# Attention with a post-norm and a quantised FFN: probabilities divided in three PSUM row buffers, rotary products taken from PSUM, no swap DMAs

## The chip, the cores and the metric

One NeuronCore of a Trainium2 chip runs the whole program in one launch. The metric is the device time of one execution in microseconds. The kernel before takes 2369.5 us (median of 3 executions, 2362.24 to 2372.11).

## The reference

```python
def layer(x, Wq, bq, Wk, bk, Wv, bv, Wo, bo, gate/up/down int8 weights and scales):   # x: (4, 1024, 256) f32
    q, k, v = heads(x @ Wq + bq) * 128 ** -0.5, heads(x @ Wk + bk), heads(x @ Wv + bv)  # 16 heads of 128
    q = q * cos + rotate_half(q) * sin          # rotate_half: (-second half, first half) of the 128 dims
    k = k * cos + rotate_half(k) * sin
    attn = softmax(causal(q @ k.T))             # 1024 x 1024 per head
    x = layernorm(x + (attn @ v) @ Wo + bo)
    return layernorm(x + ((silu(x @ Wg * sg) * (x @ Wu * su)) @ Wd) * sd)
```

There are 4 x 16 = 64 heads. The time is in them: the last 220 us are the FFN.

## The kernel before

**Precision by halves.** Matrix products are made in a fast rounded format. So each operand is kept as a rounded high part and the low rest, and each product is three matmuls (high x high, high x low, low x high). The high part is made by ScalarE (a copy that rounds), the low part by VectorE or GpSimd (the value less the high part). Probabilities and V use float16 parts, scaled by powers and bounds; the rest uses rounded float32.

**The loop.** `sequence_timelines` calls `run(n, ...)` once per head n = -1 ... 64 on every engine; each engine has its own copy of the loop body, written out by hand in 8 slots s = 0 ... 7. Every engine does its instructions in order; semaphores join them. During head n, slot s works on the 128-query row block s of head n (s+1 blocks of 128 keys, causal), and beside it lie the projections of head n+1 (s < 4), the product with V of head n-1 (`ATTEND`), and, once per pair of heads, the V projection and the output projection.

**A row block.** TensorE makes the scores in a PSUM buffer S[s % 2] of two banks (L1139). VectorE adds the mask and takes the negated maximum, and writes the row to SBUF, `p_row` (L878). ScalarE takes Exp in place with its row sum (L686), then writes the high part of the undivided probabilities, times 2^15, to `planes` (L694). VectorE writes the low part from `p_row` and `planes` (L888). A DMA on SyncE's queue transposes `planes` into `PT` (L393, `turn`), of which there are three planes in turn. The S buffer is free as soon as L878 has read it.

**The product with V.** `attend` (L1103) gathers in PSUM O[g], g = 0, 1 for the two halves of 512 queries. The division by the row sums comes here: `reciprocal` (L936, L939) makes four columns at a time, SyncE sends them to DRAM (L401) and spreads them back over all partitions as `recip_b` (L406), and `normalise_output` (L906) multiplies O[g] by it into `norm_o`. ScalarE rounds that (L528, `output_high`) and GpSimd makes the rest (L482).

**The projections and the rotary part.** `chunk` (L1156) makes a 128 x 512 piece of q or k of the next head in the upper bank of S[c % 2]. ScalarE adds the bias and takes it to SBUF, `rot` (`chunk_out`, L702). SyncE copies the two halves of 64 partitions crosswise into `swap` by two DMAs (L384, `swap_halves`). GpSimd multiplies `swap` by the sine (L452), VectorE `rot` by the cosine (L929), GpSimd adds them (L444), ScalarE rounds the sum into QK (L528) and GpSimd makes the rest (L468).

**The other PSUM users.** V pieces go through bank PJ (L1173; read by ScalarE L614 and VectorE L897), the output projection through WP (L1121; added to `resid` by VectorE L922). The bound for V's scale and the fold of bv into bo are small matmuls in WP.

## Time and profile before

| | |
|---|---|
| median of 3 executions | 2369.5 us |
| the profiled execution, and its span | 2372.22 us, 2370.4 us |
| busy TensorE, VectorE, ScalarE, GpSimd | 1929.0, 1984.0, 1375.0, 1619.6 us |
| mean granted TensorE clock | 0.908 of 2.4 GHz |
| mean busy share of the 16 DMA engines over the heads | 0.69 |

How to read it: "busy" is the union of an engine's instructions; instructions issued back to back overlap by about 0.1 us in the records, so sums of durations come out a little higher than the busy time. "Idle before" is the time in which an engine had nothing to do just ahead of an instruction, and the arrow names what ended it. The scores of head 0 start at 31.0 us, those of head 63 end soon after 2150 us.

### The profile page before, as it was taken

The page shows a single profiled execution, that of the slowest core. Times are in us where ns is not written, and L with a number is a line of the kernel's source. Part 1 is how long each engine was busy: PE and PEld are TensorE (multiplying, and loading weights), DVE is VectorE, ACT ScalarE, POOL GpSimd, SP SyncE. Part 2 cuts the span into 40 slices and gives each one's busy share as a digit, 9 for nine tenths or more (in the row PEclk, how much of TensorE's full clock was granted, in tenths as well). Part 3 has the DMA queues.
Part 4 walks back from the last instruction along what each step waited for, and adds up shares of the span by engine and source line. Part 5 has one row for each costly group of instructions (what it writes and reads, how often), then busy time and mean ns, then how long its engine had stood idle before and what let it go on. Part 6 is the DMA issues. An engine that isn't in the chain of part 4 may idle for free. (4 is left out here: it accounts for less than half of the span.)

```text
span 2370.4 us, 35295 instructions
## 1 busy us (share of the span) xinstructions
PE 1929.0 (81%) x10464; PEld 1515.4 (64%) x10464; DVE 1984.0 (84%) x2981; ACT 1375.0 (58%) x2718; POOL 1619.6 (68%) x1169
## 2 busy tenths in 40 slices
PE   5787887877888888878888878778888878878998
PEld 4566666656666666656666666656666656656887
DVE  6788888888888888888888888888888888985786
ACT  3655565655665665655666656565666656664443
POOL 4567766766677767777777777676667766773554
PEclk9899898899988998889888899889988998999999
DMA  4766777667767776767666677667766787664001
GB/s 113 175 131 125 144 156 128 128 146 152 135 134 144 139 160 133 140 139 156 142 137 135 137 157 145 127 139 151 139 132 132 144 174 150 134 125 98 19 19 36
DMA packets 716092, 311.09 MB, mean 131 GB/s; under 512 B 638080, under 2 KB 650880, under 8 KB 714496
## 3 DMA queue, kind: packets, MB, share of 16 engines
q1 hardware_dynamic: 692224, 266.88, 56.8%
q10 hardware_dynamic: 23680, 41.95, 6.4%
q8 instruction: 87, 1.43, 0.3%
q14 instruction: 101, 0.83, 0.1%
HBM read 81.95 MB, written 8.65 MB: 38 GB/s over the span
## 5 line engine op out<-in xcount | busy, mean ns | idle before, releaser
L686 ACT ACTIVATE p_row<-p_row,neg_max 128x128 f32<-128x128 f32 (+7 forms) x512 | 396.1, 774 | 598.5 <-DVE neg_max L878 589.6
L888 DVE SCALAR_TENSOR_TENSOR planes<-p_row,planes 128x128 f16<-128x128 f32 (+7 forms) x512 | 644.2, 1258 | 42.9 <-ACT planes L694 42.8
L452 POOL TENSOR_TENSOR swap<-swap,sin_t 128x512 f32<-128x512 f32 x256 | 383.5, 1499 | 217.3 <-DMA swap<-rot 217.2
L878 DVE CUSTOM_DVE_ANT_0 p_row<-S,mask_row 128x128 f32<-128x128 f32 (+7 forms) x512 | 385.0, 752 | 132.8 <-PE S L1139 116.1
L929 DVE TENSOR_TENSOR rot<-rot,cos_t 128x512 f32<-128x512 f32 x256 | 353.0, 1379 | 105.8 <-DMA swap<-rot 100.1
L444 POOL TENSOR_TENSOR rot<-rot,swap 128x512 f32<-128x512 f32 x252 | 351.4, 1394 | 71.5 <-DVE rot L929 71.4
L694 ACT ACTIVATE planes<-p_row 128x128 f16<-128x128 f32 (+7 forms) x512 | 347.3, 678 | 25.6 <-DMA PT<-planes 17.5
L1139 PE MATMUL S<-QKA 128*128 128x512 f32 (+4 forms) x1152 | 287.6, 378 | 75.8 <-issue 43.8
L1173 PE MATMUL PJ<-WV,xT 128*128 128x256 f32 x1500 | 234.1, 313 | 109.5 <-DVE VB L897 53.5
L1139 PE MATMUL S<-QKB 128*128 128x512 f32 (+4 forms) x1152 | 303.5, 394 | 16.0 <-ACT rot L702 9.2
L1173 PEld LDWEIGHTS PJ<-WV,xT 128*128 128x128 f32 x1500 | 221.7, 218 | 134.6 <-DVE VB L897 62.6
L1139 PEld LDWEIGHTS S<-QKA 128*128 128x128 f32 x1152 | 196.4, 197 | 119.9 <-issue 93.7
L1121 PE MATMUL WP<-WO,OTA 128*128 128x256 f32 x768 | 152.9, 313 | 145.9 <-DVE resid L922 134.7
L1103 PE MATMUL O<-PT,VB 128*128 128x512 f16 (+3 forms) x1152 | 242.0, 345 | 6.0 <-DMA PT<-planes 6.0
L1139 PEld LDWEIGHTS S<-QKB 128*128 128x128 f32 x1152 | 213.6, 212 | 51.9 <-issue 21.2
L1103 PE MATMUL O<-PT,VA 128*128 128x512 f16 (+3 forms) x1152 | 240.2, 343 | 4.8 <-DMA PT<-planes 4.8
L1121 PEld LDWEIGHTS WP<-WO,OTA 128*128 128x128 f32 x768 | 127.1, 214 | 165.2 <-issue 158.8
L1156 PE MATMUL S<-xT,WA 128*128 128x512 f32 x768 | 211.9, 414 | 10.5 <-DVE xT L738 8.8
L468 POOL TENSOR_TENSOR QKB<-rot,QKB 128x512 fp32r<-128x512 f32 x128 | 206.9, 1623 | 18.8 <-ACT QKB L528 18.8
L468 POOL TENSOR_TENSOR QKA<-rot,QKA 128x512 fp32r<-128x512 f32 x124 | 207.5, 1674 | 13.1 <-ACT QKA L528 12.6
L1156 PE MATMUL S<-xT,WB 128*128 128x512 f32 x768 | 202.4, 399 | 9.7 <-ACT rot L702 9.7
L702 ACT ACTIVATE rot<-S,bias_m 128x512 f32<-128x512 f32 x256 | 172.4, 674 | 25.5 <-PE S L1156 19.3
(142 smaller groups left out, 3156.7 us busy)
## 6 DMA issues: line engine op xcount, KB each, us to landing
swap<-rot SPq DMA_DIRECT2D x512, 128.0 KB, 2.6
recip_b<-recip_d SPq DMA_DIRECT2D x128, 256.0 KB, 4.1
w_raw<-in_w_heads ACTq DMA_DIRECT2D x64, 256.0 KB, 3.0
wv_raw<-in_w_heads ACTq DMA_DIRECT2D x32, 256.0 KB, 2.7
PT<-planes SPq DMA_TRANSPOSE x512, 3.7
wo_raw<-in_wo_heads ACTq DMA_DIRECT2D x32, 256.0 KB, 3.0
attn_d<-resid ACTq DMA_DIRECT2D x4, 1024.0 KB, 5.5
x_raw<-in_x_cols SPq DMA_DIRECT2D x3, 1024.0 KB, 6.0
```

What stands on the lines that cost most here:

```text
L444: nc.gpsimd.tensor_tensor(rot[:, c, :], rot[:, c, :], swap[:, c, :], ALU.add).then_inc(rot_done, 1)
L452: nc.gpsimd.tensor_tensor(swap[:, c, :], swap[:, c, :], sin_t[:, half], ALU.mult).then_inc(sin_done, 1)
L468: nc.gpsimd.tensor_tensor(q[:, c % 2, 1, half], rot[:, c, :], q[:, c % 2, 0, half].bitcast(F32), ALU.subtract).then_inc(rot_lo, 1)
L686: nc.scalar.activation(row, row, ACT.Exp, bias=neg_max[:, s:s + 1], scale=-1.0, accum_out=row_sum[:, s:s + 1]).then_inc(exped, 1)
L694: nc.scalar.activation(row_halves(n, s)[:, 0], p_row[:, k % 2, 0:cols].rearrange("p (j q) -> p j q", q=P), ACT.Copy, scale=UP).then_inc(hi ...
L878: nc.vector.tensor_tensor_reduce(row_view(p_row[:, k % 2, 0:cols], s), score_view(S[s % 2], s), row_view(mask_row[:, N - cols:], s), -1.0, ...
L888: nc.vector.scalar_tensor_tensor(halves_of[:, 1], p_row[:, k % 2, 0:cols].rearrange("p (j q) -> p j q", q=P), UP, halves_of[:, 0], ALU.mul ...
L929: nc.vector.tensor_tensor(rot[:, c, :], rot[:, c, :], cos_t[:, half], ALU.mult).then_inc(cos_done, 1)
L1103: last = mm(O[g][:, first * P:], V[buf][:, pv, j, who], PT[g][:, j, pp, first:, :].rearrange("p i q -> p (i q)"), start=j == 0 and z == 0, ...
L1139: last = mm(S[s % 2][:, z * GQ:z * GQ + b - a], QK[par][:, 0, part_q, s * P:(s + 1) * P], QK[par][:, 1, part_k, a:b], start=(part_q, part_ ...
L1156: last = mm(S[c % 2][:, GQ:], W[nxt][:, c % 2, pw, t, :], xT[:, px, t, half], start=i == 0 and t == 0, stop=i == 2 and t == KT - 1)
L1173: last = mm(v_psum(n, i)[:, t2, :], xT[:, px, t, tok], WV[:, pw, t, :, :].rearrange("p h c -> p (h c)"), start=z == 0 and t == 0, stop=z = ...
```

## The change

What it does: (1) there are three S buffers of two banks, used in turn by row number (`row_psum`), and one bank O and one bank X in place of O0, O1, WP and PJ. (2) Exp writes into the row's S buffer, no longer in place in SBUF; the reciprocal is taken per row block, 128 x 1, right after Exp, and the division is in the scale of the high part and of the low part, both read from PSUM. So S is held from the scores until the low part is made. (3) `normalise_output`, the DRAM round trip and GpSimd's `output_low` go; ScalarE and VectorE take the two parts straight from O. (4) The two DMAs per chunk go; ScalarE's copy of a chunk becomes two copies of 64 partitions that swap the halves, and VectorE's cosine product reads the chunk in PSUM and adds the bias. (5) The score scale moves to L878, and the bias copy goes. (6) Output projection, V pieces, fold and bound get other slots, all through X, and `ATTEND` is redistributed.

```diff
-    S = [pb("S0", N), pb("S1", N)]
-    O = [pb("O0", GQ), pb("O1", GQ)]
-    WP = pb("WP", GQ)
-    PJ = pb("PJ", GQ)
+    S = [pb(f"S{i}", N) for i in range(3)]
+    O = pb("O", GQ)
+    X = pb("X", GQ)
+    def row_psum(n, s):
+        return S[(8 * n + s) % 3]
...
-        return ({2: 2, 7: 3} if par else {5: 0, 7: 1}).get(s) if makes_v(n) else None
+        return ({1: 0, 7: 1} if par else {1: 2, 3: 3}).get(s)
...
-        slots = {1: 1, 5: 2, 6: 3} if par else {6: 0}
+        slots = {3: 2, 5: 3} if par else {5: 0, 7: 1}
...
-    ATTEND = {0: [(0, 0), (0, 1)], 1: [(0, 2), (0, 3)], 3: [(1, 0), (1, 1)], 4: [(1, 2), (1, 3), (1, 4)],
-              5: [(1, 5)], 6: [(1, 6)], 7: [(1, 7)]}
+    ATTEND = {0: [(0, 0), (0, 1), (0, 2), (0, 3)], 3: [(1, 0)], 4: [(1, 1), (1, 2), (1, 3)], 5: [(1, 4)],
+              6: [(1, 5), (1, 6), (1, 7)]}
...  SyncE: swap_halves and reciprocals are gone, turn stays
...  GpSimd: output_low is gone; WO's rest moves from slot 0 to 2, WV's from 2 to 5
-                        pool.wait_ge(swapped[c], 32 * (m + 1))
+                        pool.wait_ge(chunk_sb, 2 * n_four(m, c))
...  ScalarE, at the head of slot s: output_high in slots 1 and 7, value_high of slot s-1's piece; then
-                nc.scalar.activation(row, row, ACT.Exp, bias=neg_max[:, s:s + 1], scale=-1.0,
+                nc.scalar.activation(row_psum(n, s)[:, 0:cols], p_row[:, k % 2, 0:cols], ACT.Exp,
+                                     bias=neg_max[:, s:s + 1], scale=-1.0,
                                      accum_out=row_sum[:, s:s + 1]).then_inc(exped, 1)
...
-                act.wait_ge(exped, k + 1)
+                act.wait_ge(recip_ok, k + 1)
                 wait(act, turned_in[k % 3], 16 * (k // 3))
-                nc.scalar.activation(row_halves(n, s)[:, 0], p_row[:, k % 2, 0:cols].rearrange(
-                    "p (j q) -> p j q", q=P), ACT.Copy, scale=UP).then_inc(high, 1)
+                nc.scalar.activation(row_halves(n, s)[:, 0], row_psum(n, s)[:, 0:cols].rearrange(
+                    "p (j q) -> p j q", q=P), ACT.Copy, scale=recip[:, s:s + 1]).then_inc(high, 1)
...
-                nc.scalar.activation(rot[:, c, :], S[c % 2][:, GQ:], ACT.Identity,
-                                     bias=bias_m[:, m_par, c % 2:c % 2 + 1],
-                                     scale=SCALE if c % 2 == 0 else 1.0).then_inc(chunk_sb, 1)
+                for lo, hi in ((0, D // 2), (D // 2, 0)):
+                    nc.scalar.activation(swap[lo:lo + D // 2, c, :], row_psum(n, c)[hi:hi + D // 2, GQ:], ACT.Identity,
+                                         bias=bqk[hi:hi + D // 2, c % 2, m % H:m % H + 1]).then_inc(chunk_sb, 1)
...  VectorE, order within slot s: add_output of slot s-1's piece, masked_scores(s), probs_low(s-1),
...  output_low (s = 1, 7), value_low, reciprocal(s), scale_up, rotate_cos(s-1)
-                wait(dve, low, k - 1)
-                wait(dve, exped, n_scored(n - 1, s))
+                wait(dve, exped, k - 1)
...
-                nc.vector.scalar_tensor_tensor(halves_of[:, 1], p_row[:, k % 2, 0:cols].rearrange(
-                    "p (j q) -> p j q", q=P), UP, halves_of[:, 0], ALU.mult, ALU.subtract).then_inc(low, 1)
+                nc.vector.scalar_tensor_tensor(halves_of[:, 1], row_psum(n, s)[:, 0:cols].rearrange(
+                    "p (j q) -> p j q", q=P), recip[:, s:s + 1], halves_of[:, 0], ALU.mult, ALU.subtract
+                    ).then_inc(low, 1)
...
+            def output_low(h, g):
...
+                nc.vector.scalar_tensor_tensor(OT[q][:, 1, o], O[:, :], pv_down[:, slot:slot + 1],
+                                               OT[q][:, 0, o].bitcast(F32), ALU.mult, ALU.subtract
+                                               ).then_inc(o_lo, 1)
...
-                nc.vector.tensor_tensor(rot[:, c, :], rot[:, c, :], cos_t[:, half], ALU.mult).then_inc(cos_done, 1)
+                dve.wait_ge(chunk_sb, 2 * n_four(m, c))
+                wait(dve, rot_lo, n_four(m - 1, c))
+                nc.vector.scalar_tensor_tensor(rot[:, c, :], row_psum(n, c)[:, GQ:], bqk[:, c % 2, m % H:m % H + 1],
+                                               cos_t[:, half], ALU.add, ALU.mult).then_inc(cos_done, 1)
...
+            def reciprocal(n, s):
+                dve.wait_ge(exped, n_scored(n, s))
+                nc.vector.tensor_scalar(sum_down[:, s:s + 1], row_sum[:, s:s + 1], 1.0 / UP, None, ALU.mult
+                                        ).then_inc(summed_down, 1)
+                dve.wait_ge(summed_down, n_scored(n, s))
+                nc.vector.reciprocal(recip[:, s:s + 1], sum_down[:, s:s + 1]).then_inc(recip_ok, 1)
...  TensorE, scores(s)
-                    wait(pe, maxed, n_scored(n, s) - 2)
-                    if s >= 4:
-                        wait(pe, chunk_sb, n_four(m, s % 2 + 2) if project else 0)
+                    k = n_row(n, s)
+                    wait(pe, low, k - 2)
+                    if project and 4 <= s < 7:
+                        pe.wait_ge(cos_done, n_four(m, s - 3))
```

## Rows read from the trace of the kernel before

**Rows 1.** From the page: span, busy time, granted clock and DMA, packets.

```profile
span 2370.4 us, 35295 instructions
PE 1929.0 (81%) x10464; PEld 1515.4 (64%) x10464; DVE 1984.0 (84%) x2981; ACT 1375.0 (58%) x2718; POOL 1619.6 (68%) x1169
...
DMA packets 716092, 311.09 MB, mean 131 GB/s; under 512 B 638080, under 2 KB 650880, under 8 KB 714496
```

**Rows 2.** Busy time by stretch, ahead of, over and behind the heads.

```profile
core 0: us, PE busy (x) PEld busy (x) DVE busy (x) ACT busy (x) POOL busy (x), PEclk, DMA share, GB/s
0.00:31.00 31.00, 15.76 (x76) 13.41 (x77) 17.20 (x26) 10.31 (x18) 8.38 (x11) 0.96 0.47 143
31.00:2150.00 2119.00, 1711.40 (x9222) 1328.58 (x9222) 1805.59 (x2622) 1268.76 (x2551) 1501.26 (x1075) 0.90 0.69 141
2150.00:2370.00 220.00, 201.82 (x1169) 173.40 (x1168) 161.20 (x335) 95.97 (x151) 110.01 (x84) 0.98 0.14 38
```

**Rows 3.** Costliest groups of the page: row work and rotary work, all shapes together.

```profile
L686 ACT ACTIVATE p_row<-p_row,neg_max 128x128 f32<-128x128 f32 (+7 forms) x512 | 396.1, 774 | 598.5 <-DVE neg_max L878 589.6
L888 DVE SCALAR_TENSOR_TENSOR planes<-p_row,planes 128x128 f16<-128x128 f32 (+7 forms) x512 | 644.2, 1258 | 42.9 <-ACT planes L694 42.8
L452 POOL TENSOR_TENSOR swap<-swap,sin_t 128x512 f32<-128x512 f32 x256 | 383.5, 1499 | 217.3 <-DMA swap<-rot 217.2
L878 DVE CUSTOM_DVE_ANT_0 p_row<-S,mask_row 128x128 f32<-128x128 f32 (+7 forms) x512 | 385.0, 752 | 132.8 <-PE S L1139 116.1
L929 DVE TENSOR_TENSOR rot<-rot,cos_t 128x512 f32<-128x512 f32 x256 | 353.0, 1379 | 105.8 <-DMA swap<-rot 100.1
L444 POOL TENSOR_TENSOR rot<-rot,swap 128x512 f32<-128x512 f32 x252 | 351.4, 1394 | 71.5 <-DVE rot L929 71.4
L694 ACT ACTIVATE planes<-p_row 128x128 f16<-128x128 f32 (+7 forms) x512 | 347.3, 678 | 25.6 <-DMA PT<-planes 17.5
L1139 PE MATMUL S<-QKA 128*128 128x512 f32 (+4 forms) x1152 | 287.6, 378 | 75.8 <-issue 43.8
...
L1139 PE MATMUL S<-QKB 128*128 128x512 f32 (+4 forms) x1152 | 303.5, 394 | 16.0 <-ACT rot L702 9.2
...
L702 ACT ACTIVATE rot<-S,bias_m 128x512 f32<-128x512 f32 x256 | 172.4, 674 | 25.5 <-PE S L1156 19.3
```

**Rows 4.** Groups of VectorE, shapes apart.

```profile
L906 DVE TENSOR_TENSOR norm_o<-O,recip_b 128x512 f32<-128x512 f32 x128 | 137.7, 1076 | 0.0
L936 DVE TENSOR_SCALAR sum_up<-row_sum,pv_up 128x4 f32<-128x4 f32 x128 | 131.9, 1031 | 0.0
L878 DVE CUSTOM_DVE_ANT_0 p_row<-S,mask_row 128x512 f32<-128x512 f32 x64 | 43.6, 681 | 0.9 <-PE S L1139 0.8
L939 DVE RECIPROCAL recip<-sum_up 128x4 f32<-128x4 f32 x128 | 22.8, 178 | 4.4
```

**Rows 5.** Single lines of VectorE and GpSimd: durations in ns, least/median/most.

```profile
L897 DVE SCALAR_TENSOR_TENSOR VB<-PJ,v_up,VB x64: 720/740/774, 61.9 to 2102.1; 128x512 f16<-128x512 f32 x64
L1026 DVE SCALAR_TENSOR_TENSOR rot<-S,sg_t,swap x64: 732/750/754, 2160.6 to 2357.1; 128x512 f32<-128x512 f32 x64
L936 DVE TENSOR_SCALAR sum_up<-row_sum,pv_up x128: 217/1230/2332, 51.4 to 2155.4; 128x4 f32<-128x4 f32 x128
L764 DVE TENSOR_SCALAR pv_up<-v_up x32: 152/154/156, 28.6 to 2045.5; 128x1 f32<-128x1 f32 x32
L762 DVE RECIPROCAL v_up<-bound x32: 162/164/166, 28.4 to 2045.3; 128x1 f32<-128x1 f32 x32
L444 POOL TENSOR_TENSOR rot<-rot,swap x252: 1251/1334/2003, 43.4 to 2122.8; 128x512 f32<-128x512 f32 x126
```

**Rows 6.** Groups of ScalarE and GpSimd, shapes apart.

```profile
L614 ACT ACTIVATE VB<-PJ,v_up 128x512 f16<-128x512 f32 x64 | 42.8, 669 | 0.0
L694 ACT ACTIVATE planes<-p_row 128x512 f16<-128x512 f32 x64 | 39.7, 620 | 1.7 <-DMA PT<-planes 1.7
L551 ACT COPY bias_m<-bqk 128x2 f32<-128x2 f32 x64 | 11.4, 178 | 0.0
L468 POOL TENSOR_TENSOR QKB<-rot,QKB 128x512 fp32r<-128x512 f32 x128 | 206.9, 1623 | 18.8 <-ACT QKB L528 18.8
L482 POOL TENSOR_TENSOR OTA<-norm_o,OTA 128x512 fp32r<-128x512 f32 x64 | 82.7, 1292 | 23.9 <-ACT OTA L528 23.9
```

**Rows 7.** Who waited for whom, longest first: us in total, times, longest.

```profile
ACT p_row L686 <- DVE neg_max L878: 589.6, 356, 4.7
...
PE WP L1121 <- DVE resid L922: 134.7, 30, 7.2
...
DVE p_row L878 <- PE S L1139: 116.1, 99, 3.4
...
DVE rot L929 <- DMA swap<-rot: 100.1, 60, 7.0
...
PE PJ L1173 <- DVE VB L897: 53.5, 12, 7.2
...
PE PJ L1173 <- DVE VA L897: 37.9, 9, 4.6
```

More of the change, by code:

```diff
@@ L369, in run @@
                             sp.dma_start(dst, src).then_inc(rows_in, 16)
-                    if prev and s in (1, 3):
-                        reciprocals(n - 1, 1, s == 1)
-                    if own and s in (5, 7):
-                        reciprocals(n, 0, s == 5)
                     if s == 0 and own and n % H == H // 2 and n < HEADS - H:
@@ L453, in run @@
                                                 ALU.mult).then_inc(sin_done, 1)
-                    if par == 0 and s == 2 and own and makes_v(n):
+                    if par == 0 and s == 5 and own and makes_v(n):
                         pool.wait_ge(wv_hi, (n >> 1) + 2)
@@ L653, in run @@
                         act.dma_start(resid[:, 0:NT, :], attn_d[0]).then_inc(attn_in, 16)
-                    if s == 3 and par == 1 and own:
+                    if s == 6 and par == 1 and own:
                         wait(act, WO_lo, (n - 1) >> 1)
@@ L659, in run @@
                                       ).then_inc(WO_in, 16)
-                    if s == 7 and par == 1 and own:
-                        wait(act, wo_made, 2 * (n - 1))
-                        act.wait_ge(WO_in, 8 * (n + 1))
+                    if s == 1 and par == 0 and prev:
+                        wait(act, wo_made, 2 * (n - 2))
+                        act.wait_ge(WO_in, 8 * n)
                         copy(WO[:, :, 0, :], wo_raw[:, :, :]).then_inc(WO_hi, 1)
@@ L757, in scale_up @@
                 dve.wait_ge(bounded, pair + 1)
-                wait(dve, recip_ok, n_group(2 * pair - 3, 1))
                 nc.vector.tensor_scalar(bound[:, :], bound_psum, 1e-30, 1.0 / UP, ALU.max, ALU.mult
@@ L823, in run @@
                         probs_low(n, s - 1)
[L824 to L832 removed]
+                    if s == 1 and prev:
+                        output_low(n - 1, 0)
@@ new lines, in run @@
+                    if s == 7 and prev:
+                        output_low(n - 1, 1)
+                    if n < 0 and s == 4:
+                        scale_up(0)
+                    if s > 0:
+                        value_low(n, par, v_group(n, par, s - 1))
+                    elif n >= 0:
+                        value_low(n - 1, 1 - par, v_group(n - 1, 1 - par, 7))
+                    if own:
+                        reciprocal(n, s)
+                    if own and makes_v(n) and par == 0 and s == 6:
+                        scale_up((n >> 1) + 1)
@@ new lines, in run @@
+                    if project and 1 <= s < 5:
+                        rotate_cos(n, m, s - 1)
+                    if n < 0 and 2 <= s < 6:
+                        c = s - 2
+                        dve.wait_ge(sin_done, n_four(m, c))
+                        dve.wait_ge(cos_done, n_four(m, c))
+                        nc.vector.tensor_tensor(rot[:, c, :], rot[:, c, :], swap[:, c, :],
+                                                ALU.add).then_inc(rot_done, 1)
+                    if own and makes_v(n) and par == 0 and s == 3:
@@ L1102, in attend @@
                 for z, (pv, pp) in enumerate(((0, 0), (1, 0), (0, 1))):
-                    last = mm(O[g][:, first * P:], V[buf][:, pv, j, who],
+                    last = mm(O[:, first * P:], buf[:, pv, j, who],
                               PT[g][:, j, pp, first:, :].rearrange("p i q -> p (i q)"),
@@ L1150, in chunk @@
                         pe.wait_ge(x_lo, n_x(m >> 4, c // 2))
-                    wait(pe, maxed, n_scored(n, c) - 2 if own else n_scored(n - 1, 7))
-                    if c >= 2:
-                        pe.wait_ge(chunk_sb, n_four(m, c) - 2)
+                    if n == 0 and c == 0:
+                        pe.wait_ge(cos_done, n_four(0, 3))
+                    if c == 3:
+                        pe.wait_ge(cos_done, n_four(m, 0))
                     for i, (pw, px) in enumerate(((0, 0), (0, 1), (1, 0))):
                         for t in range(KT):
-                            last = mm(S[c % 2][:, GQ:], W[nxt][:, c % 2, pw, t, :], xT[:, px, t, half],
+                            last = mm(row_psum(n, c)[:, GQ:], W[nxt][:, c % 2, pw, t, :], xT[:, px, t, half],
                                       start=i == 0 and t == 0, stop=i == 2 and t == KT - 1)
```

332 lines of the change are left out of this document (138 added, 194 removed).

## The prediction

> **What bounds the kernel now.** I read the stretches first [rows 2]: 31 us of lead-in, 2119 us of heads, 220 us of FFN. The diff works on the heads, so the unit of this text is one head: 2119 / 64 = 33.1 us. Divided by 64 in the same way, VectorE is busy 1805.6 / 64 = 28.2 us, TensorE 1711.4 / 64 = 26.7 us, GpSimd 1501.3 / 64 = 23.5 us, ScalarE 1268.8 / 64 = 19.8 us. No engine is full: VectorE comes first at 85%, TensorE second at 81%.
>
> The costliest groups [rows 3] show why VectorE leads. Its low part of the probabilities takes 1258 ns where the masked maximum, over the same columns, takes 752. The first reads two tensors in SBUF, the second one in PSUM and a mask row. The cosine product of 512 columns, again from two tensors in SBUF, takes 1379 ns; a product of the same size with one operand in PSUM takes 740 to 750 [rows 5]. And a tensor_scalar over four columns takes from 217 to 2332 ns [rows 5]. So these instructions are not slow by their size; they stand still. GpSimd shows the other side: one and the same sum takes 1251 to 2003 ns [rows 5]. VectorE and GpSimd hold each other up, where VectorE's instruction has both inputs in SBUF or is a small tensor_scalar between SBUF tiles. In the Trainium skill, the page "SBUF — State Buffer" (Who interferes with whom) gives that rule: the two share a pair of ports that one of them holds for a whole instruction, and a VectorE instruction with one SBUF input outside the two-port modes keeps clear of it. The trace agrees, by the rows just named.
>
> Next the waits [rows 7]. ScalarE's 589.6 us for the masked maximum is an idle engine waiting for a loaded one: 9.2 us per head. TensorE waits 134.7 us for an addition to `resid` to free WP and 53.5 + 37.9 us for V's low part to free PJ: both hang on where VectorE is in its queue. VectorE itself waits for scores (116.1 us) and for the swap DMAs (100.1 us). So the period of 33.1 us is VectorE's 28.2 and 4.9 us in which it waited, mostly for things that themselves stood behind VectorE.
>
> **VectorE, part by part, per head.** (a) Low part of the probabilities, now from PSUM and float16 in SBUF, with a pointer scalar: that is the form of V's low part, 740 ns at 512 columns [rows 5], where the masked maximum has 681 [rows 4], 59 ns less. So 8 x (752 + 59) = 6.5 us in place of 8 x 1258 = 10.1 us: 3.6 us less. (b) Four cosine products: 4 x 1.379 = 5.5 us become 4 x 0.75 = 3.0 (the FFN's product of PSUM, a pointer scalar and an SBUF tile [rows 5]): 2.5 less. (c) Two normalisations of 1.076 [rows 4] become two low parts of O at 0.74: 0.7 less. (d) Two wide reciprocals, 2 x (1.031 + 0.178) = 2.4 us [rows 4], go, and eight narrow ones come. The narrow pair is 154 + 164 ns [rows 5], 8 x 0.318 = 2.5 us: 0.1 more. Sum: 28.2 - 3.6 - 2.5 - 0.7 + 0.1 = 21.5 us. Bounds: if reading PSUM did not help at all, (a) to (c) bring nothing and VectorE stays at 28.3; if the narrow tensor_scalar stands still like the wide one, at 1.031 us, it adds 8 x 0.877 = 7.0 us. I take the low values, because the rows for them are of the same form and hardly spread (720 to 774, 732 to 754, 152 to 156).
>
> The narrow one is the point where a rule could speak against the change. What the rows show: 128 x 4 spreads over 217 to 2332 ns in 128 executions, 128 x 1 over 152 to 156 in 32, at a place where GpSimd is busy two thirds of the time. In the Trainium skill, the page "VectorE: DVE Perf Modes" (Mode 2×_2P) lets a tensor_scalar use both ports only when its outermost dimension of more than one element can be halved; 128 x 1 has none, and so would stay clear. Row and rule agree; had the rule caught it, the third rival below would be the forecast.
>
> **ScalarE.** Eight copies of 64 partitions in place of four of 128: a copy's time goes by its columns, so I take 0.674 us [rows 3] for each: 4 x 0.674 = 2.7 us more. Half of that, if the partitions counted, would be nothing more: 0 is the lower bound. The high part of the probabilities takes its scale from a pointer and its input from PSUM: 669 ns in the form of V's copy against 620 [rows 6], 8 x 0.05 = 0.4 more. The bias copy, 11.4 / 64 = 0.2 [rows 6], goes. Exp now writes to PSUM; the nearest rows (669 from PSUM, 620 in SBUF) differ by 0.05 us, so 0 +/- 0.4 us per head; I take 0. ScalarE: 19.8 + 2.7 + 0.4 - 0.2 = 22.7 us. It now also waits for the reciprocal between Exp and high part. For s < 4 the two chunk copies (1.35 us) cover that; for the other four rows it is 0.32 us and the way there and back, some 0.35: 1.4 us. ScalarE's own sequence is thus 24.1 us long.
>
> The price of that sequence lies in the order of the two queues. In a slot VectorE does masked(s), low(s-1), reciprocal(s); ScalarE does Exp(s), chunk copies, high(s). Behind the reciprocal, which waits for Exp(s), VectorE queues the cosine product and the next masked maximum, for which ScalarE waits. Exp(s) (0.77 us) is covered by low(s-1) (0.81 us), so VectorE loses little. Back to the next Exp it is 0.32 + 0.75 + 0.75 + 0.77 us, 2.6 us per slot, less than ScalarE's 24.1 / 8 = 3.0. So the alternation is not longer than ScalarE's own work.
>
> **GpSimd.** The two low parts of O go: (82.7 us [rows 6], and the same again for the other head parity) / 64 = 2.6 us. The twelve rotary instructions of a head (1499, 1394 and 1623 ns [rows 3, 6]) no longer meet a VectorE instruction that holds them up; at 1292 [rows 6] they lose 4 x (0.21 + 0.10 + 0.33) = 2.6 us. 23.5 - 5.2 = 18.3 us; bound above 20.9. It is last of the four and off the path.
>
> **SyncE and the DMAs.** 8 swap DMAs and 4 small ones per head go, and with them most of the 638,080 packets under 512 B [rows 1]. What gains is the wait for them (100.1 us of VectorE, 217.2 us of GpSimd [rows 3, 7]). SyncE's queue keeps the transposes alone; they waited for VectorE, and TensorE hardly ever for them, so a faster DMA brings nothing by itself.
>
> **TensorE.** The matmuls are the same: 26.7 us per head at a mean granted clock of 0.90, against 0.98 in the FFN [rows 2]. The two levels are 1.2 and 2.4 GHz, so the mean 0.90 means a fifth of the heads' time at the low one. If the clock became what the FFN has, the same work is 26.7 x 0.90 / 0.98 = 24.5 us. TensorE idles 6.4 us per head now.
>
> Its new wait: scores(s) wait for the low part of row s-3, not the maximum of row s-2, and chunk, products with V, output and V pieces stand behind scores(s) in its queue. One row holds a buffer for scores (287.6 + 303.5) / 512 = 1.15, maximum 0.75, Exp 0.77, reciprocal 0.32, high 0.73, low 0.81 us, 4.6 with the ways between. Three buffers and eight rows allow each row 28 x 3 / 8 = 10.5 us. That leaves 5.9 us, nearly two slots, for standing in queues; so the ring as such does not bind. The single X bank is tighter: each of its users waits until VectorE, one slot later, has emptied it. With VectorE's slot shorter by a quarter, (28.2 - 21.5) / 28.2, and no DMA in its way, I keep a quarter of TensorE's 6.4 us idle: 1.6 us.
>
> **The sum.** TensorE 26.7 is now first, ahead of ScalarE 24.1, VectorE 21.5 and GpSimd 18.3. Period 26.7 + 1.6 = 28.3 us. Time of heads 64 x 28.3 = 1811 us, in place of 2119. Lead-in and FFN keep 31 + 220 us (their changed slots are worth a few us either way). Span 2062 us, and by the profiled execution's 2372.22 against 2370.4 us 2064; that execution lies 2.7 us above the median, so 2061 us.
>
> **Rivals.** First rival: the engines hand over as loosely as before. Then the ratio of period to the fullest engine stays 33.1 / 28.2 = 1.17, and 26.7 x 1.17 = 31.3 us; 64 x 31.3 + 251 = 2254 us. For it: three engines close to full, in strict order, one X and one O bank where four were. Against: a good part of the old waits were DMAs and VectorE's long instructions. Chance 0.24.
>
> Second rival: TensorE, idling less, gets the FFN's clock, 24.5 us, and the bound is ScalarE's 24.1 and it together, 25.8 us with the same 1.3 to 1.6 of idling: 64 x 25.8 + 251 = 1902 us. For it: the clock of rows 2 is higher where TensorE is busier. Chance 0.14.
>
> Third rival, slower: the narrow tensor_scalar waits for GpSimd as the wide one does. It stands eight times per head between Exp and high part, where ScalarE waits for it, and ahead of everything of the next slot. 28.3 + 7.0 = 35.3 us, 64 x 35.3 + 251 = 2510 us. It decides from (33.1 - 28.3) / 8 = 0.6 us per row on. For it: the 1031 ns of rows 4. Against: the 32 narrow ones of rows 5. Chance 0.07.
>
> Fourth rival: the change does not do what it says, VectorE's instructions stay as long with a PSUM operand as they were, and the DMAs were hidden. VectorE 28.3 us with the waits for the swap gone (100.1 / 64 = 1.6 us): 33.1 + 0.1 - 1.6 = 31.6 less ScalarE's longer copies in the alternation, which may take it all back: 2275 to 2370 us. Chance 0.05, half of it within 0.5% of before.
>
> **How the numbers follow.** The forecast has 0.50, for 2061 us and 1980 to 2140 around it (a period of 27.0 to 29.5). Range: from 1950, which takes in the better half of the way to the second rival, to 2255, the first rival, with little over 0.2 left out. A measurement of this kernel tells 0.5% from no change; faster by more than that 0.50 + 0.24 + 0.14 + 0.02, say 0.90, within it 0.02, slower 0.08.
>
> **What would show it.** Right: L888's successor has about 810 ns on average, the cosine product 750, the narrow tensor_scalar under 200 with no spread; no "swap" DMA; the three GpSimd groups near 1290; VectorE at 21 to 22 us per head, TensorE at over 90% of the period, and the waits of ScalarE for the maximum below a third of 589.6 us. Wrong: TensorE waiting for the low part (the ring) or for additions and V parts (X) by more than 3 us per head; half-partition copies or Exp that take longer than 0.67 and 0.77 us; a narrow tensor_scalar near 1 us.

## The result and the profile after

The changed kernel takes 1922.26 us (1920.36 to 1923.27, 4 runs) against 2370.69 us for the kernel before beside it: ratio 0.8114, 95% interval 0.8093 to 0.8134. The forecast was 2061 us, the range 1950 to 2255 us. The direction was right, the gain is 448 us where 308 were forecast, and the time lies 28 us below the range, next to the second rival's 1902 us.

The page of the changed kernel, the lines that answer to [rows 1]:

```profile
span 1918.6 us, 33748 instructions
PE 1778.1 (93%) x10464; PEld 1406.3 (73%) x10464; DVE 1573.9 (82%) x3748; ACT 1591.1 (83%) x2910; POOL 1246.2 (65%) x1041
...
DMA packets 638257, 210.01 MB, mean 109 GB/s; under 512 B 609408, under 2 KB 622208, under 8 KB 636672
```

The stretches of the changed kernel, as in [rows 2] (window, busy time of each engine, TensorE's granted clock, DMA share, GB/s):

```profile
31.00:1700.00 1669.00, 1556.32 (x9192) 1214.81 (x9191) 1393.10 (x3373) 1476.19 (x2730) 1132.68 (x949) 0.99 0.59 119
1700.00:1918.00 218.00, 202.00 (x1173) 174.06 (x1171) 159.52 (x338) 97.95 (x154) 105.31 (x81) 0.98 0.13 37
```

All of the gain is in the heads; the stretch behind them takes 218 us, 220 before. A head takes 1669 / 64 = 26.1 us, where it took 33.1. Per head, TensorE is busy 24.3 us (26.7 before), VectorE 21.8 (28.2), ScalarE 23.1 (19.8), GpSimd 17.7 (23.5). The clock over the heads rose from 0.90 to 0.99 with the matmuls unchanged. The packets fell by only 78,000: the transposes' queue alone has 614,400 of the 638,257 that are left, so the prediction was wrong that most of the small ones go with the swap.

The groups of the changed kernel that answer to [rows 3]:

```profile
L848 DVE SCALAR_TENSOR_TENSOR planes<-S,recip,planes 128x128 f16<-128x128 f32 (+7 forms) x512 | 417.3, 815 | 94.0 <-ACT planes L657 91.2
L657 ACT ACTIVATE planes<-S,recip 128x128 f16<-128x128 f32 (+7 forms) x512 | 379.0, 740 | 129.8 <-DVE recip L899 115.9
L423 POOL TENSOR_TENSOR swap<-swap,sin_t 128x512 f32<-128x512 f32 x256 | 331.3, 1294 | 190.4 <-ACT swap L665 190.2
L648 ACT ACTIVATE S<-p_row,neg_max 128x128 f32<-128x128 f32 (+7 forms) x512 | 380.0, 742 | 51.7 <-DVE neg_max L838 44.5
L838 DVE CUSTOM_DVE_ANT_0 p_row<-S,mask_row 128x128 f32<-128x128 f32 (+7 forms) x512 | 385.1, 752 | 27.8 <-PE S L1112 26.3
L417 POOL TENSOR_TENSOR rot<-rot,swap 128x512 f32<-128x512 f32 x252 | 323.0, 1282 | 72.4 <-DVE rot L889 69.8
L665 ACT ACTIVATE swap<-S,bqk 64x512 f32<-64x512 f32 x512 | 349.8, 683 | 18.7 <-DVE wmax L706 5.9
...
L889 DVE SCALAR_TENSOR_TENSOR rot<-S,bqk,cos_t 128x512 f32<-128x512 f32 x256 | 192.0, 750 | 2.9 <-ACT swap L665 2.9
```

Two things are to be seen. The durations are close to those of the prediction: low part 815 ns (810 forecast), cosine product 750 (750), half-partition copy 683 (674), GpSimd 1282 to 1294 (1292). And the waits have moved: ScalarE's for the masked maximum fell from 589.6 to 44.5 us. In its place each of VectorE and ScalarE now waits for the other. So every sign that the prediction named for being right came, with VectorE at 21.8 us and TensorE at 93% of the period, and the time still lies outside: none of the signs looked at the clock. The narrow tensor_scalar of the changed kernel (ns: least/median/most), which answers to the wide one of [rows 5]:

```profile
L896 DVE TENSOR_SCALAR sum_down<-row_sum x512: 133/153/156, 29.8 to 1704.3; 128x1 f32<-128x1 f32 x171
```

### The profile page after: what moved, and what is told of

Its sections match the earlier page's. It is cut to its first block and busy times, and to the rows that moved or that the text cites. A ratio compares the mean times of both kernels' runs of the same rounds, so it can differ in the third digit from the quotient of the medians.

```text
span 1918.6 us, 33748 instructions
## 1 busy us (share of the span) xinstructions
PE 1778.1 (93%) x10464; PEld 1406.3 (73%) x10464; DVE 1573.9 (82%) x3748; ACT 1591.1 (83%) x2910; POOL 1246.2 (65%) x1041
## 2 busy tenths in 40 slices
DMA packets 638257, 210.01 MB, mean 109 GB/s; under 512 B 609408, under 2 KB 622208, under 8 KB 636672
## 3 DMA queue, kind: packets, MB, share of 16 engines
q1 hardware_dynamic: 614400, 165.91, 45.2%
## 5 line engine op out<-in xcount | busy, mean ns | idle before, releaser
L848 DVE SCALAR_TENSOR_TENSOR planes<-S,recip,planes 128x128 f16<-128x128 f32 (+7 forms) x512 | 417.3, 815 | 94.0 <-ACT planes L657 91.2
L657 ACT ACTIVATE planes<-S,recip 128x128 f16<-128x128 f32 (+7 forms) x512 | 379.0, 740 | 129.8 <-DVE recip L899 115.9
L423 POOL TENSOR_TENSOR swap<-swap,sin_t 128x512 f32<-128x512 f32 x256 | 331.3, 1294 | 190.4 <-ACT swap L665 190.2
L648 ACT ACTIVATE S<-p_row,neg_max 128x128 f32<-128x128 f32 (+7 forms) x512 | 380.0, 742 | 51.7 <-DVE neg_max L838 44.5
L838 DVE CUSTOM_DVE_ANT_0 p_row<-S,mask_row 128x128 f32<-128x128 f32 (+7 forms) x512 | 385.1, 752 | 27.8 <-PE S L1112 26.3
L417 POOL TENSOR_TENSOR rot<-rot,swap 128x512 f32<-128x512 f32 x252 | 323.0, 1282 | 72.4 <-DVE rot L889 69.8
L665 ACT ACTIVATE swap<-S,bqk 64x512 f32<-64x512 f32 x512 | 349.8, 683 | 18.7 <-DVE wmax L706 5.9
L439 POOL TENSOR_TENSOR QKA<-rot,QKA 128x512 fp32r<-128x512 f32 x124 | 160.1, 1291 | 122.3 <-ACT QKA L491 122.1
L1152 PEld LDWEIGHTS X<-WV,xT 128*128 128x128 f32 x1500 | 193.7, 190 | 29.7 <-DVE VB L858 10.2
L1152 PE MATMUL X<-WV,xT 128*128 128x256 f32 x1500 | 208.2, 288 | 6.9 <-DVE VA L858 3.5
L889 DVE SCALAR_TENSOR_TENSOR rot<-S,bqk,cos_t 128x512 f32<-128x512 f32 x256 | 192.0, 750 | 2.9 <-ACT swap L665 2.9
L1063 PEld LDWEIGHTS O<-PT,VB 128*128 128x128 f16 x1152 | 99.8, 100 | 118.1 <-issue 55.2
L1063 PEld LDWEIGHTS O<-PT,VA 128*128 128x128 f16 x1152 | 99.2, 99 | 116.6 <-issue 53.6
```

Of the source, the lines that this page charges most:

```text
L417: nc.gpsimd.tensor_tensor(rot[:, c, :], rot[:, c, :], swap[:, c, :], ALU.add).then_inc(rot_done, 1)
L423: nc.gpsimd.tensor_tensor(swap[:, c, :], swap[:, c, :], sin_t[:, half], ALU.mult).then_inc(sin_done, 1)
L439: nc.gpsimd.tensor_tensor(q[:, c % 2, 1, half], rot[:, c, :], q[:, c % 2, 0, half].bitcast(F32), ALU.subtract).then_inc(rot_lo, 1)
L648: nc.scalar.activation(row_psum(n, s)[:, 0:cols], p_row[:, k % 2, 0:cols], ACT.Exp, bias=neg_max[:, s:s + 1], scale=-1.0, accum_out=row_su ...
L657: nc.scalar.activation(row_halves(n, s)[:, 0], row_psum(n, s)[:, 0:cols].rearrange("p (j q) -> p j q", q=P), ACT.Copy, scale=recip[:, s:s ...
L665: nc.scalar.activation(swap[lo:lo + D // 2, c, :], row_psum(n, c)[hi:hi + D // 2, GQ:], ACT.Identity, bias=bqk[hi:hi + D // 2, c % 2, m % ...
```

## The experiments

All times stand beside runs of the kernel before on the same chip; ratios are to those, with 95% intervals. "Per head" is the stretch from 31 us to 220 us ahead of the end, divided by 64.

**e1, the rotary part alone, in the kernel before.**

```diff
+ for lo, hi in ((0, D // 2), (D // 2, 0)):        # ScalarE, as in the change; no swap DMAs
+     nc.scalar.activation(swap[lo:lo + D // 2, c, :], S[c % 2][hi:hi + D // 2, GQ:], ACT.Identity, ...)
...
- rotate_cos(c, m)        # VectorE, slot c + 2, rot and cos_t in SBUF, waits for the swap
+ rotate_cos(s - 1, m)    # slot c + 1, reads S[c % 2][:, GQ:] in PSUM, waits for ScalarE
```

Two things come with it: TensorE waits for the cosine product, no longer for the copy, before it writes the S buffer again, and the score scale moves to the masked maximum.

> The kernel before with the rotary part of the change alone: ScalarE's two copies of 64 partitions swap the halves, VectorE's cosine product reads the chunk in PSUM, no swap DMAs; all else (two S buffers, Exp and low part in SBUF, reciprocals through DRAM) as before. Theory (VectorE's length and its waits set the period, and TensorE's clock follows TensorE's idling): VectorE loses 2.5 us of work and 1.6 us of DMA waits per head, so the period falls from 33.1 to about 29.5 to 31 us, 2140 to 2240 us in all, with a clock of 0.92 to 0.95. Rival (the row chain through SBUF is the bound, the swap DMAs were hidden): 2340 us or more, clock 0.90.

Measured: 2034.51 us (2028.06 to 2034.81), ratio 0.8561 (0.8538 to 0.8585), clock 0.969. This part by itself brings 340 us, more than the theory gave it.

**e5, the kernel before without the swap.** GpSimd multiplies `rot` by the sine straight away, VectorE waits for that product.

```diff
- pool.wait_ge(swapped[c], 32 * (m + 1))
- nc.gpsimd.tensor_tensor(swap[:, c, :], swap[:, c, :], sin_t[:, half], ALU.mult)
+ pool.wait_ge(chunk_sb, n_four(m, c))
+ nc.gpsimd.tensor_tensor(swap[:, c, :], rot[:, c, :], sin_t[:, half], ALU.mult)
...
- dve.wait_ge(swapped[c], 32 * (m + 1))
+ dve.wait_ge(sin_done, n_four(m, c))
```

The halves are not exchanged here, so the kernel leaves out the rotary part.

> The kernel before without the swap of the halves: the two DMAs per chunk go, and GpSimd multiplies rot itself by the sine (so the rotary part is left out of the output's meaning). VectorE's cosine product stays in SBUF with two SBUF inputs and waits for GpSimd's product in place of the DMA; ScalarE's copies stay four per head. Theory A (what the rotary part of the change brings is the DMAs' latency in the chain chunk, swap, sine, sum, rounding): most of the 340 us, 2050 to 2150 us. Theory B (it is the cosine product's standing still for GpSimd, 2.5 us of VectorE per head): 100 us or less, 2270 us or more.

Measured: 2316.04 us (2313.49 to 2317.58), ratio 0.978 (0.9756 to 0.9803), clock 0.914. The swap DMAs are worth 54 us while the cosine product keeps its slot and waits for GpSimd's product in their place. The busy times of e5 and e1 over the heads, one row each, e5 first:

```profile
31.00:2092.00 2061.00, 1689.87 (x9209) 1326.96 (x9208) 1637.44 (x2619) 1268.83 (x2546) 1381.89 (x1074) 0.91 0.55 113
```

```profile
31.00:1813.00 1782.00, 1607.39 (x9215) 1243.69 (x9214) 1615.27 (x2619) 1469.76 (x2798) 1468.38 (x1074) 0.97 0.66 130
```

VectorE is busy alike, 25.6 and 25.2 us per head, and ScalarE does less in e5; yet a head takes 32.2 us in e5 and 27.8 in e1. So VectorE's load is not what separates them. (It is alike by way of two differences: the cosine product takes 1303 ns in e5 and 746 in e1, the low part of the probabilities 947 and 1205.) In e5 VectorE sits in front of the cosine product and waits for the sine, with the masked maxima of the next rows behind it:

```profile
L928 DVE TENSOR_TENSOR rot<-rot,cos_t x256: 677/1671/2756, 16.9 to 2060.8; 128x512 f32<-128x512 f32 x128
its engine sat idle before it (us, times) until:
  POOL swap L451: 160.8, 135
who waited for it (us, times):
  POOL rot L442: 236.3, 247
```

What that does to the row work is seen in ScalarE's wait for the masked maximum: 668.9 us in e5, 393.4 in e9 and 232.3 in e1.

**e9, e1 with the cosine product's operand back in SBUF.** Same slots, no DMA, ScalarE's eight copies per head; the halves are not exchanged, so the rotary part is left out again.

```diff
+ for into in (rot, swap):
+     nc.scalar.activation(into[:, c, :], S[c % 2][:, GQ:], ACT.Identity, ...)
...
- nc.vector.scalar_tensor_tensor(rot[:, c, :], S[c % 2][:, GQ:], bias_m[...], cos_t[:, half], ALU.add, ALU.mult)
+ nc.vector.tensor_tensor(rot[:, c, :], rot[:, c, :], cos_t[:, half], ALU.mult)
```

> Experiment e1 with one thing put back: ScalarE writes the chunk twice over 128 partitions, into rot and into swap (its load is e1's; the halves are not swapped, so the rotary part is left out of the output's meaning), and VectorE's cosine product reads rot in SBUF, in e1's slot. No DMA, same queue orders as e1. Theory A (the operand's place is what counts: with two SBUF inputs the product stands still for GpSimd, 1.3 us in place of 0.75): 2150 us or more. Theory B (what counts is the slot: the product one slot earlier and waiting for ScalarE alone, no longer for the swap or the sine): within 60 us of e1's 2034 us.

Measured: 2181.45 us (2180.63 to 2183.12), ratio 0.9206 (0.9175 to 0.9237), clock 0.966. From e1 it is 147 us, from e5 135 us the other way. The cosine product in e9:

```profile
L927 DVE TENSOR_TENSOR rot<-rot,cos_t x256: 675/1119/2718, 15.9 to 1923.3; 128x512 f32<-128x512 f32 x128
its engine sat idle before it (us, times) until:
  ACT swap L701: 3.2, 3
who waited for it (us, times):
  PE S L1156: 143.1, 78
  PE S L1137: 96.4, 112
```

The operand's place reached a second instruction too. The low part of the probabilities, whose code is the same in both kernels, first in e1 and then in e9:

```profile
L887 DVE SCALAR_TENSOR_TENSOR planes<-p_row,planes 128x128 f16<-128x128 f32 (+7 forms) x512 | 617.1, 1205 | 43.8 <-ACT planes L692 42.8
```

```profile
L887 DVE SCALAR_TENSOR_TENSOR planes<-p_row,planes 128x128 f16<-128x128 f32 (+7 forms) x512 | 711.2, 1389 | 66.8 <-ACT planes L692 63.9
```

It costs VectorE 1.5 us per head, as much as the cosine product's own 1.4 (1102 ns on average against 746).

So the 340 us divide into 54 for the DMAs, 135 for the earlier slot and the wait for ScalarE alone, and 147 for the operand in PSUM, which makes 336; the rest lies within the difference of the runs of the kernel before. The 135 are a lower bound, since that step also carries ScalarE's extra copies, and a head became shorter although VectorE is busy 2.4 us longer in it. The time of e9 lies in the range of theory A, but half of the way from e5 to e1 is theory B's: neither covers it alone. The 147 may be too much for the operand: e9 keeps e1's wait of TensorE for the cosine product, which an operand in SBUF does not call for, and it is 143.1 + 96.4 = 239.5 us there against 100.1 + 23.7 = 123.8 in e1. No run takes that wait out.

**e2, the changed kernel with its rotary part undone** (one copy, two swap DMAs, cosine product from SBUF in slot c + 2).

> The changed kernel with its rotary part undone: one copy of a chunk by ScalarE, two swap DMAs, cosine product from SBUF one slot later. Theory: VectorE 21.8 + 2.5 = 24.3 us, GpSimd longer by its collisions, ScalarE 2.7 us shorter. VectorE becomes about as full as TensorE: period 27 to 28 us, 1980 to 2050 us, clock 0.96 to 0.98. Rival (ScalarE's copies were the bound beside TensorE, DMAs hidden): no change or faster, 1880 to 1930 us.

Measured: 2077.66 us (2072.64 to 2079.22), ratio 0.8743 (0.8716 to 0.877), clock 0.971. 155 us slower than the changed kernel, although ScalarE does 2.9 us less per head; GpSimd waits 535.7 us for the swap. A little beyond the theory's end; the rival (ScalarE's copies cost more than they bring) fell.

**e3, Exp in place in SBUF, high and low part from there.**

```diff
- nc.scalar.activation(row_psum(n, s)[:, 0:cols], p_row[:, k % 2, 0:cols], ACT.Exp, ...)
+ nc.scalar.activation(p_row[:, k % 2, 0:cols], p_row[:, k % 2, 0:cols], ACT.Exp, ...)
```

> The changed kernel, but Exp goes in place in SBUF and high and low part are read from there; the S buffer is held as long as in the changed kernel. Only where the probabilities lie differs. Theory (VectorE with two inputs in SBUF stands still for GpSimd): the low part goes from 815 ns back to 1150 to 1300, VectorE 21.8 + 3 = 25 us, GpSimd's groups back to 1400 to 1700 ns, period 28 to 29.5 us, 2040 to 2140 us, clock near 0.95. Rival (the place does not matter, the ring and order do): under 1950 us.

Measured: 2009.28 us (2003.66 to 2011.75), ratio 0.8458 (0.8435 to 0.8482), clock 0.974. The durations went back as expected, the low part to 1196 ns and GpSimd's rounding rest to 1658 (QKA) and 1481 (QKB):

```profile
L849 DVE SCALAR_TENSOR_TENSOR planes<-p_row,recip,planes 128x128 f16<-128x128 f32 (+7 forms) x512 | 612.3, 1196 | 67.8 <-ACT planes L657 64.3
```

The time rose by 87 us, less than expected: 3 us more in VectorE's low parts cost 1.4 us per head.

**e4, the narrow tensor_scalar made 128 x 4.**

```diff
- nc.vector.tensor_scalar(sum_down[:, s:s + 1], row_sum[:, s:s + 1], 1.0 / UP, None, ALU.mult)
+ nc.vector.tensor_scalar(sum_down[:, s, :], row_sum[:, s, :], 1.0 / UP, None, ALU.mult)   # 4 columns
```

> The changed kernel with the narrow tensor_scalar ahead of the reciprocal made 128 x 4, the form of the kernel before, eight per head as the narrow one; its three added columns are constants. Third rival of the prediction, priced: if a tensor_scalar of four columns between SBUF tiles waits for GpSimd, it takes about 1 us in place of 0.15, on the way between Exp and high part: 5 to 7 us per head, 2240 to 2370 us. If the 1031 ns before came from something else (what stood around it there), the time stays within 20 us of the changed kernel.

Measured: 2089.59 us (2084.67 to 2093.41), ratio 0.8799 (0.8775 to 0.8823), clock 0.956. All else equal, three more columns in a tiny instruction cost 167 us. Its group:

```profile
L897 DVE TENSOR_SCALAR sum_down<-row_sum 128x4 f32<-128x4 f32 x512 | 230.0, 449 | 88.4 <-ACT S L648 85.6
```

449 ns on average where the narrow one has 149; its median is 171 and its longest 1275 ns, so it stands still only at times. A head takes 1840 / 64 = 28.8 us, 2.7 more, and 8 x 0.30 = 2.4 us of that is the instruction itself: it is paid in full, since ScalarE waits for it between Exp and high part. The third rival's mechanism exists; its size was a third of what the prediction gave (0.30 us each in place of 0.88). Why it is smaller was not tested: GpSimd's instructions are shorter here, and the place in the queue is another.

**e6, useless matmuls added to the kernel before**, where TensorE waits for an addition to `resid`.

```diff
+ if made and s == 6 and par == 1 and n < HEADS:
+     pe.wait_ge(o_norm, n_group(n - 1, 0))
+     for z in range(3):
+         mm(O[0][:, :], ones[:, :], cos_t[:, 0:GQ], start=True, stop=True)
```

> The kernel before with work added: three float32 matmuls of 512 columns into a free PSUM bank, whose result nobody reads, ahead of the last output projection of each pair, where TensorE waits 4.5 us for an addition. Theory (TensorE's low clock comes from its idling, and costs time): the granted clock rises by 0.02 or more and the time stays or falls, 2300 to 2375 us. Rival (the clock does not hang on idling, or its level does not matter while VectorE is the bound): clock 0.91 and 2370 to 2420 us.

Measured: 2331.6 us (2321.55 to 2340.5), ratio 0.9845 (0.9807 to 0.9884), clock 0.936 over the execution. More work, 38 us less time, 1.6%. TensorE's wait for the addition fell from 134.7 us to 62.4. The heads of e6, and the group of added matmuls:

```profile
31.00:2119.00 2088.00, 1749.65 (x9411) 1327.65 (x9411) 1807.24 (x2622) 1269.02 (x2551) 1501.93 (x1075) 0.93 0.69 143
```

```profile
L1199 PE MATMUL O<-cos_t,ones 128*128 128x512 f32 x186 | 84.9, 593 | 0.0
```

Without the added ones TensorE was busy (1749.7 - 84.9) / 64 = 26.0 us per head, where [rows 2] have 26.7: the same matmuls went faster, at a clock of 0.93 in place of 0.90. VectorE, ScalarE and GpSimd each changed by less than 2 us over all the heads. So filling TensorE's idle time raised its clock, and that reached the time. The share of idle time alone does not give the clock, though. e9:

```profile
31.00:1960.00 1929.00, 1638.16 (x9212) 1247.21 (x9211) 1793.79 (x2620) 1403.76 (x2800) 1527.08 (x1074) 0.97 0.60 120
```

TensorE is busy 85% of this stretch at 0.97; in e4 it is busy 88% at 0.95, in e6 84% at 0.93. And e9 has a head of 30.1 us at 0.97, so a high clock does not make a short head by itself.

**e7, VectorE loaded in the changed kernel.**

```diff
  reciprocal(n, s)
+ nc.vector.tensor_reduce(spare[:, s:s + 1], cos_t[:, 0:608], AX.X, ALU.max).then_inc(spared, 1)
```

> The changed kernel with work added on VectorE: after each reciprocal a maximum over 608 columns of the cosine table (one SBUF input, about 0.78 us) that nobody reads, so that VectorE has 28 us per head as in the kernel before. If the prediction's sum is right in kind (period = fullest engine + 1.5 to 2 us), the period is 29.5 to 30 us, 2140 to 2170 us, and TensorE idles 15% with a clock of 0.94 to 0.96. If what made the kernel before slow was VectorE's load as such, 33 us, 2370 us. If the load hides in VectorE's waits, under 2000 us.

Measured: 2083.31 us (2082.3 to 2085.38), ratio 0.8799 (0.8778 to 0.882), clock 0.962. VectorE was busy 1675.83 / 64 = 26.2 us per head, not 28: each added maximum took 767 ns, but it overlaps the instructions ahead of and behind it by nearly 0.1 us each in the records. Its 4.4 us more cost 2.5 us of a head (28.6 us). That is between the ranges expected: part of the load hid in waits, part did not. Hence even with VectorE near its old load a head takes 4.5 us less than before.

**e8 and e10, TensorE and ScalarE relieved in the changed kernel; e14, both.** e8 leaves out the third product in V pieces and output projection (`for a, b in ((0, 0), (0, 1))`); e10 has one copy of a chunk over 128 partitions (`nc.scalar.activation(swap[:, c, :], row_psum(n, c)[:, GQ:], ...)`), so e10 and e14 leave out the exchange of the halves.

> The changed kernel with the third product (low part of the stationary operand) left out of V pieces and output projection: 16 of 48 matmuls of 256 columns per head go, about 2.0 us of TensorE. If TensorE is the bound, the period falls by 1.2 to 2.0 us, 1795 to 1845 us. If ScalarE (23.1 us busy and its waits for the reciprocal) is it, the time falls by less than 30 us.

> The changed kernel with one copy of 128 partitions per chunk in place of two of 64 (the halves are not swapped, so the rotary part is left out of the output's meaning): 2.7 us less of ScalarE per head. A lighter TensorE (e8) gave 14 us. If ScalarE's sequence is the bound of the changed kernel: period down by 1 to 1.5 us until TensorE's 24.3 us bind, 1830 to 1860 us. If neither alone is the bound: less than 30 us as in e8.

> The changed kernel with both e8 (third product left out of V pieces and output projection) and e10 (one copy of 128 partitions per chunk, halves not swapped): the rotary part and a part of the precision are left out. TensorE 22.3 us, ScalarE 20.4 us, VectorE 21.7 us per head. If TensorE and ScalarE bound the changed kernel side by side, each hiding the other: more than the sum 14 + 34 us, 1800 to 1840 us. If it is VectorE and its alternation with ScalarE: 1865 to 1885 us.

Measured: e8 1908.02 us (1906.25 to 1910.34), ratio 0.8059 (0.8035 to 0.8082); e10 1888.14 us (1887.46 to 1889.93), ratio 0.7969 (0.7936 to 0.8001); e14 1873.01 us (1870.95 to 1881.32), ratio 0.7925 (0.7891 to 0.796). Heads of e8 and of e14:

```profile
31.00:1686.00 1655.00, 1455.84 (x8175) 1102.89 (x8174) 1384.12 (x3365) 1472.78 (x2726) 1130.10 (x949) 0.98 0.59 120
```

```profile
31.00:1650.00 1619.00, 1463.07 (x8187) 1115.39 (x8186) 1376.10 (x3366) 1278.82 (x2473) 1131.48 (x949) 0.97 0.61 122
```

TensorE loses 1.6 us of busy time in e8 and a head 0.2; ScalarE loses 3.1 us in e10 and a head 0.5; the two gains add (14 + 34 and 49 us). In e14 TensorE is at 22.9 us, ScalarE at 20.0, VectorE at 21.5, of a head of 25.3. Neither TensorE's load nor that of ScalarE's chunk copies bounds the changed kernel. Where e10's 3.1 us went is seen in ScalarE's waits:

```profile
ACT S L648 <- DVE neg_max L837: 158.2, 191, 2.1
ACT planes L657 <- DVE recip L898: 157.8, 318, 0.7
```

They are 44.5 and 115.9 us in the changed kernel, so of the 3.1 us taken from ScalarE 2.4 came back as waits for VectorE.

**e11 and e12, two versions meant to be faster; e13, both.** e11 drops the factor 2^15, so that one reciprocal per row is left; e12 rounds the weights on GpSimd.

```diff
- nc.vector.tensor_scalar(sum_down[:, s:s + 1], row_sum[:, s:s + 1], 1.0 / UP, None, ALU.mult)
- nc.vector.reciprocal(recip[:, s:s + 1], sum_down[:, s:s + 1])
+ nc.vector.reciprocal(recip[:, s:s + 1], row_sum[:, s:s + 1])
...
+ nc.gpsimd.tensor_copy(W[buf][:, q, 0, :, :]..., w_raw[:, q, :, :]...).then_inc(w_hi, 1)   # and WV, WO
```

> The changed kernel without the factor 2^15 on the probabilities: the narrow tensor_scalar goes, one reciprocal per row is left, pv_down loses its 1/2^15. 8 x 0.15 = 1.2 us less of VectorE per head, and 0.15 to 0.2 us less of ScalarE's wait in the rows where it waits (115.9 us in all, 257 times): 257 x 0.17 = 44 us at most; 1875 to 1915 us. If TensorE is the bound: 1920 us.

> The changed kernel with the rounding of the weights (2 copies of 256 columns per head, 2 of 512 per pair) moved from ScalarE to GpSimd, which waits 190 us for ScalarE ahead of its first sine product and has 8 us per head idle. ScalarE 1.4 us less per head, GpSimd 2 us more. If ScalarE is the bound: 60 to 90 us less, 1830 to 1860 us; if it is shared with TensorE: 1880 to 1905 us. If GpSimd's copies meet VectorE's or come late for the chunks: 1930 us or more.

> The changed kernel with both e11 (one reciprocal per row, no factor 2^15) and e12 (weights rounded by GpSimd). e11 brought 37 us, e12 49 us. If the engines' handing over is the bound, the gains add for the most part: 1835 to 1855 us. If TensorE, already 95% busy in e12, is the bound behind them: 1855 to 1873 us.

Measured: e11 1885.69 us (1885.12 to 1887.49), ratio 0.7958 (0.7931 to 0.7985); e12 1873.42 us (1870.56 to 1873.79), ratio 0.7902 (0.7875 to 0.793); e13 1846.48 us (1843.77 to 1849.11), ratio 0.7802 (0.7778 to 0.7826). e13 beats both kernels: 76 us less than the changed one, and the gains add for the most part (37 + 49 and 76 us). The time of e12 lies between the two ranges expected, below "shared with TensorE" and above "ScalarE is the bound". e12 takes only (1476.2 - 1410.3) / 64 = 1.0 us per head from ScalarE and a head falls by (1669 - 1621) / 64 = 0.75, where e10's 3.1 us gave 0.5. What e12 takes stands mostly in slots 4 to 6, where ScalarE waits for each reciprocal, what e10 takes in slots 0 to 3, where it covers that wait. That the place makes the difference is a reading of the two, not shown: e12 also shortens GpSimd's waits. In e13 TensorE is busy 96% of the span:

```profile
PE 1770.0 (96%) x10464; PEld 1409.7 (76%) x10464; DVE 1475.9 (80%) x3236; ACT 1528.0 (83%) x2725; POOL 1327.7 (72%) x1226
```

## Why the prediction was wrong

**Right: the durations and three of the four loads.** VectorE 21.5 us forecast and 21.8 measured, ScalarE 22.7 and 23.1, GpSimd 18.3 and 17.7. Two figures of ScalarE were off in opposite directions: Exp into PSUM takes 742 ns in place of 774 (0.26 us less per head, within the bounds given), the high part 740 in place of 678 (0.5 more; 0.4 forecast). The high part's 62 ns are two effects against each other: e3 has it from SBUF with the same scale from a pointer at 776 ns, so the pointer costs 98 ns over the constant scale of the kernel before, and reading PSUM gives 36 back. In the Trainium skill, "ScalarE: Activation LUTs" (Step-by-step: what each stage is for) says that ScalarE reaches PSUM sooner than SBUF as a destination; the 32 ns agree with it, and so does e3, where Exp into SBUF takes 767 ns in the changed kernel's order.

**The step that failed: TensorE's 26.7 us per head.** The sum took TensorE's busy time at the clock of 0.90, and put 1.6 us of idling on it. The prediction had the term that mattered, 26.7 x 0.90 / 0.98 = 24.5 us, and gave it to a rival with a chance of 0.14. Measured are 24.3 us at 0.99, so the whole measured head, 26.1 us, is shorter than the term that was to be its first. The step treated the clock as a given. e6 shows, in the kernel before, that it rises when TensorE's waits are filled; in the changed kernel no run holds the clock down with the waits left as they are, so how much of the 448 us came through it is not shown. The idling itself was near: 1.8 us against 1.6. With the right first term the same sum gives 24.5 + 1.6 = 26.1 us, the measured head. That this number comes out is luck, for the next point.

**Also wrong: that the fullest engine is the bound.** e8 shows that TensorE is not it, though it is busy 93% of the time. What the runs point to is the alternation of VectorE and ScalarE, each waiting for the other's piece of a row, which the prediction weighed and passed over as "not longer than ScalarE's own work". The waits of VectorE and of ScalarE in the changed kernel (us in total, times, longest), those between the two:

```profile
DVE planes L848 <- ACT planes L657: 91.2, 223, 3.2
DVE sum_down L896 <- ACT S L648: 81.3, 211, 4.2
...
DVE OTA L866 <- ACT OTA L625: 17.1, 60, 0.6
```

```profile
ACT planes L657 <- DVE recip L899: 115.9, 257, 0.7
...
ACT S L648 <- DVE neg_max L838: 44.5, 83, 1.5
```

VectorE idles (1669 - 1393) / 64 = 4.3 us per head, of which at least (91.2 + 81.3 + 17.1) / 64 = 3.0 for ScalarE. ScalarE idles (1669 - 1476) / 64 = 3.0 us, of which 2.5 for VectorE. The 257 waits for the reciprocal are one for each row with s >= 4 (64 x 4 = 256), as forecast; they cost 0.45 us each, not 0.35. So ScalarE's own sequence is 23.1 + 1.8 = 24.9 us long, 24.1 forecast, and the alternation is longer than the 2.6 us per slot of the prediction. One slot of the changed kernel, from Exp of row block 4 to Exp of row block 5 (lines of ScalarE's timeline, then of VectorE's, then of ScalarE's; start and duration in us):

```profile
1012.79 0.79 ACT L648 ACTIVATE S<-p_row,neg_max 128x640 f32<-128x640 f32 x1
1013.51 0.19 ACT L648 ACTIVATION_READ_ACCUMULATOR S<-p_row,neg_max 128x1 f32 x1
...
1013.73 0.15 DVE L896 TENSOR_SCALAR sum_down<-row_sum 128x1 f32<-128x1 f32 x1 [0.34 <-ACT S L648]
1013.92 0.16 DVE L899 RECIPROCAL recip<-sum_down 128x1 f32<-128x1 f32 x1
1014.00 0.75 DVE L889 SCALAR_TENSOR_TENSOR rot<-S,bqk,cos_t 128x512 f32<-128x512 f32 x1
1014.90 0.96 DVE L838 CUSTOM_DVE_ANT_0 p_row<-S,mask_row 128x768 f32<-128x768 f32 x1 [0.15 <-PE S L1112]
...
1015.90 0.91 ACT L648 ACTIVATE S<-p_row,neg_max 128x768 f32<-128x768 f32 x1 [0.47 <-DVE neg_max L838]
```

It takes 3.1 us. The prediction's sum had means over all rows, 0.75 for the masked maximum where this row takes 0.96, and left out the reading of Exp's row sum (0.19 us) and the wait for the scores (0.15). e4 and e11 confirm from both sides that this path counts: lengthening the step between Exp and high part by 0.30 us per row costs 2.7 us per head, shortening it by the 0.15 us instruction gives (1669 - 1633) / 64 = 0.6 us. e8, e10 and e14 (small gains that add) speak against one load as the bound; which single wait comes first over a whole head was not settled.

**The first rival** (31.3 us, the old looseness carried over) fell: the changed kernel has 26.1 us over a fullest engine of 24.3, a ratio of 1.07, and e7 has VectorE at 26.2 us and a head at 28.6, a ratio of 1.09 against 1.17 before. The looseness was in the old order. e1, e5 and e9 show what it was made of: a cosine product that waited in VectorE's queue, in front of the next rows, for something two engines away. **The second rival**, 1902 us, came nearest in time and had the clock right; its other half, TensorE and ScalarE as the bound together, is not what e8, e10 and e14 show. **The fourth rival** fell by the durations above. **The third** was real in kind (e4) and did not strike, because one column was used.

**What the prediction gave too little: the order of the queue.** It priced the rotary part at 2.5 us of VectorE and 1.6 us of DMA waits, 4.1 us per head. Alone in the kernel before it brings 5.3 us (33.1 to 27.8, e1), of which the DMAs are 0.9 (e5), the slot 2.1 or more (e9), and the operand 2.3 or less.
